# When the carried row is taken, and for how many chunks an x row is gathered ahead

## The chip, the core and the metric

The kernel runs on one core of one Trainium2 chip. The time is that of the whole program on the device, in microseconds. Of the kernel before there are three runs, 3502.38 to 3505.12 us, with a median of 3504.13 us.

## The reference

12,500 nodes with 256 features each, 212,500 edges sorted by destination (100,000 in both directions and one loop per node). What is computed, cut to what matters:

```
x1 = layernorm(x);  h = (x1 @ W) as 4 heads x 64;  a_src, a_dst = sums of h with two vectors, per head
alpha = leaky_relu(a_src[src] + a_dst[dst], 0.2)
alpha = exp(alpha - max over the edges of dst);  alpha /= sum over the edges of dst
out   = sum over the edges of dst of alpha * h[src]           # 12,500 x 256
x     = x + relu(layernorm(out + bias) * gamma + beta)
x     = x + mixture of experts(layernorm(x))                  # two of 8 experts for all rows, 256 -> 512 -> 256
```

## The kernel before

**First stage.** 50 pairs of blocks of 128 rows are loaded, transposed, multiplied with W and the attention columns, scaled by the row's norm and stored as a table in DRAM: 4 x (64 features and a one), a one, a_src and a_dst, 269 floats a row. While this runs, GpSimd gathers, for the first X_CHUNKS = 74 chunks, the rows of x that the last tile of the chunk needs (gather_x, L736, 128 rows of 1 KB), and SyncE stores them, three chunks at a time, in the DRAM tensor x_src (store_x, L534). pair_ahead(c) says which pair's transposes (tick T* of TensorE) the gather of chunk c waits for: (c - 2) * 2 // 3. SyncE stores a part 5 pairs later; the parts left over are stored after the last pair.

**Second stage.** The edges lie in 119 chunks of 14 tiles of 128 edges. A step works on several chunks at once: "own" (the messages of this step's chunk), "prev" (the chunk before is closed), "ahead", "far" (later chunks are prepared) and up to five steps ahead for the x rows. Ticks in angle names: a * marks work for the chunk ahead, a ^ for the one two ahead. There are 116 full steps in a row; the loop body holds four of them. In a step:

- GpSimd (L781) gathers the table rows of the chunk ahead, one indirect DMA per tile. In the first rounds of the walk (X_ROUNDS = 17 rounds of four) it is 13 tiles (GATHERS), since the 14th tile's rows are not fetched but computed; later it is all 14. Ahead of row 0 it waits for the messages and for TensorE's expand* of three steps before, ahead of row 6 (FIRST_ROW) for TensorE's lT^ of two steps before, the transpose of the attention values of the chunk gathered last.
- The x row: SyncE loads 128 rows from x_src (xe, L573); TensorE transposes them (xT, L911) into psXT, one half in bank 5 beside the carried row, one in bank 6; ScalarE copies them (xT, L1177); in the next step TensorE multiplies with W (xrow, L901) and ScalarE writes the scaled result as the 14th tile (xrow, L1169). VectorE and ScalarE make the norm (xstat, xvar, xln, xrstd).
- ScalarE, in this order: oh_b* (one-hots, two activations, L1098), we, we_act (L1120), carry (L1125), msgs0 (8 activations, L1105), asrc^ (L1137, waits until the rows have landed), msgs (8), rexp (L1147), acc (L1151), carried (4 activations, L1155), oh* (two, L1098), xrow, xT, wself, selfm, and the small ones of two layer norms.
- VectorE: edge_v (L1437) to DMIN, LAST_*, five messages msg0 to msg4 (L1406) with r_t (L1485) ahead of msg4, then wcur^, r_sc, newseg^, r_mn, node^, r_d1, r_d, pen^ (L1504), node_v (L1508, waits for lT^), RUNMAX^, LASTMAX^, MTILE*, the one-hots ohT0^ and ohT^ (L1401) with MNODE* and AD* between, SHIFT*, merged0 to merged3 (L1553) with LO* between, den, rden, biased0 to 3 (L1573), st (L1580), mv, gam (L1588), normed, xmid (L1597).
- TensorE: nodemax* (L881), the own node's message and the last four tiles' sums (agg, L888 and L874), lT^ (L894), xrow, xT, lastT^ (L917), turned^ (14 transposes, L922), expand* (14 matmuls, L929), the sums of the first ten tiles (half, L874), router (L942), carry (L947).

The carried row: where a node's edges run over the end of a chunk, the last row of the sums (TensorE's carry, in bank 5) is taken by ScalarE (carry), rescaled with factors that VectorE makes from it (r_t, r_sc, r_mn, r_d1, r_d), of which ScalarE takes the exponential (rexp), multiplied (carried) and added to the first row of the next chunk's sums (merged0 to 3).

The order is written out by hand. Each engine counts its instructions on one semaphore (Ticks), and a wait names a tick and a step. The list of names in Ticks is the order in which an engine does them.

**Third stage.** Two experts, in 24 groups of 512 rows and one rest.

## Time and profile before

| | |
|---|---|
| median of three runs | 3504.13 us |
| the profiled execution: its own time | 3474.59 us |
| its span, first to last instruction | 3472.8 us |
| busy: TensorE, VectorE, ScalarE, GpSimd | 2494.7, 2261.4, 1741.6, 1606.7 us |
| mean granted clock of TensorE | 0.855 |
| table gathers of GpSimd | 1594, 958 ns each |

A busy time is a sum over the span. "Idle before" in a group is the time for which the engine stood still just ahead of that group's instructions, and behind the arrow stands what released most of it. "remote" means that the profile shows no releaser; "issue" that the engine waited for nothing that it shows. "L111 q" is a sequencer's count of left-out ticks. A matmul in single precision is two instructions.

### The profile page before, as it was taken

The page shows a single profiled execution, that of the slowest core. Times are in us where ns is not written, and L with a number is a line of the kernel's source. Part 1 is how long each engine was busy: PE and PEld are TensorE (multiplying, and loading weights), DVE is VectorE, ACT ScalarE, POOL GpSimd, SP SyncE. Part 2 cuts the span into 40 slices and gives each one's busy share as a digit, 9 for nine tenths or more (in the row PEclk, how much of TensorE's full clock was granted, in tenths as well). Part 3 has the DMA queues.
Part 4 walks back from the last instruction along what each step waited for, and adds up shares of the span by engine and source line. Part 5 has one row for each costly group of instructions (what it writes and reads, how often), then busy time and mean ns, then how long its engine had stood idle before and what let it go on. Part 6 is the DMA issues. An engine that isn't in the chain of part 4 may idle for free. (4 is left out here: it accounts for less than half of the span.)

```text
span 3472.8 us, 66576 instructions
## 1 busy us (share of the span) xinstructions
PE 2494.7 (72%) x13162; PEld 1809.5 (52%) x13162; DVE 2261.4 (65%) x9525; ACT 1741.6 (50%) x5715; POOL 1606.7 (46%) x1689
## 2 busy tenths in 40 slices
PE   7746666766666766666666666666666699999998
PEld 6534445555554555454444444444444466666666
DVE  5446676766766667676666666666666655655555
ACT  4436666666665666665655555555555422222221
POOL 5465555655655656555666666666666000000000
PEclk9858888887778888888888888888888799999999
DMA  8944444444444444444444444444445201111110
GB/s 282 325 130 129 130 136 133 134 134 131 133 131 129 135 135 134 131 133 131 133 130 130 132 131 131 132 133 133 132 130 128 68 31 37 39 39 38 37 36 33
DMA packets 238971, 415.86 MB, mean 120 GB/s; under 512 B 67998, under 2 KB 153502, under 8 KB 238878
## 3 DMA queue, kind: packets, MB, share of 16 engines
q0 software_dynamic: 80064, 229.34, 24.9%
q1 hardware_dynamic: 157462, 184.01, 16.3%
q10 hardware_dynamic: 1351, 1.62, 0.2%
q14 instruction: 79, 0.64, 0.1%
q8 instruction: 15, 0.25, 0.0%
HBM read 361.68 MB, written 53.13 MB: 119 GB/s over the span
## 5 line engine op out<-in xcount | busy, mean ns | idle before, releaser
L781 POOL DMA_INDIRECT rows<-table,idx x1594 | 1526.3, 958 | 1008.6 <-issue 404.0
L874 PE MATMUL bank<-msg,oh 128*128 128x260 f32 x3332 | 984.7, 451 | 115.4 <-issue 99.4
L874 PEld LDWEIGHTS bank<-msg,oh 128*128 128x128 f32 x3332 | 750.5, 230 | 287.8 <-issue 134.1
L1105 ACT ACTIVATE msg<-rows,we 128x65 f32<-128x65 f32 x1904 | 478.6, 333 | 0.4
L1406 DVE TENSOR_TENSOR msg<-rows,bank 128x520 f32<-128x520 f32 x595 | 382.3, 677 | 0.6 <-DVEq L111 0.3
L992 PE MATMUL bank<-rows,msg 128*128 128x256 f32 x1536 | 340.6, 378 | 0.0
L979 PE MATMUL bank<-rows 128*128 128x512 f32 x768 | 335.8, 595 | 2.6 <-DMA rows<-in_L_ffn_W 2.6
L1098 ACT ACTIVATE oh_b<-bank 128x896 bf16<-128x896 bf16 x238 | 205.3, 914 | 244.3 <-remote 226.4
L922 PE MATMUL bank<-ident_b,ohT 128*128 128x128 bf16 x1666 | 178.8, 289 | 199.0 <-DVE acc L1553 52.0
L1241 ACT ACTIVATE msg<-bank,b_sb 128x512 f32<-128x512 f32 (+1 forms) x200 | 134.4, 679 | 364.4 <-PE bank L979 346.7
L992 PEld LDWEIGHTS bank<-rows,msg 128*128 128x128 f32 x1536 | 288.4, 189 | 51.4 <-issue 10.3
L922 PEld LDWEIGHTS bank<-ident_b,ohT 128*128 128x128 bf16 x1666 | 149.7, 133 | 219.8 <-issue 124.2
L979 PEld LDWEIGHTS bank<-rows 128*128 128x128 f32 x768 | 146.0, 190 | 178.1 <-issue 174.0
L1125 ACT ACTIVATE carry<-bank 1x265 f32<-1x265 f32 x119 | 45.5, 382 | 375.9 <-remote 131.9
L894 PE MATMUL bank<-ident,asrc 128*70 128x128 f32 x238 | 60.1, 340 | 220.1 <-ACT asrc L1137 133.1
L1098 ACT ACTIVATE oh<-bank 128x896 f32<-128x896 bf16 x238 | 200.9, 891 | 0.9 <-PE bank L881 0.8
L917 PE MATMUL bank<-ident,lastmax 70*128 70x70 f32 x238 | 65.4, 370 | 182.8 <-DVE lastmax L1517 180.6
L881 PE MATMUL bank<-last_p,oh_b 128*128 128x15 bf16 x1666 | 61.1, 171 | 175.3 <-DVE last_p L1472 59.5
L1202 ACT ACTIVATE ln<-mv,eps 128x1 f32<-128x1 f32 x119 | 35.1, 295 | 280.6 <-DVE mv L1584 155.6
L881 PEld LDWEIGHTS bank<-last_p,oh_b 128*128 128x128 bf16 x1666 | 50.2, 97 | 238.2 <-ACT bank L1119 114.0
L1508 DVE TENSOR_REDUCE node_v<-bank 128x70 f32<-128x210 f32 x119 | 44.7, 376 | 197.4 <-remote 91.1
L1437 DVE TENSOR_REDUCE edge_v<-bank 128x112 f32<-128x336 f32 x119 | 60.0, 504 | 171.2 <-remote 164.0
(223 smaller groups left out, 4108.8 us busy)
## 6 DMA issues: line engine op xcount, KB each, us to landing
dst_b<-dst SPq DMA_DIRECT2D x121, 448.0 KB
rows<-table,idx POOLq DMA_INDIRECT x1594
tab_w<-table SPq DMA_DIRECT2D x120, 134.5 KB
x_w<-in_x_rows SPq DMA_DIRECT2D x120, 128.0 KB
x_mid<-x_o SPq DMA_DIRECT2D x119, 128.0 KB
table<-msg SPq DMA_DIRECT2D x50, 269.0 KB
rows<-x_mid SPq DMA_DIRECT2D x26, 512.0 KB, 3.9
msg<-in_x_rows SPq DMA_DIRECT2D x51, 256.0 KB
```

Of the source, the lines that this page charges most:

```text
L781: pool.indirect_dma_start(rows[:, slot, t, :], None, table, bass.IndirectOffsetOnAxis(ap=idx[slot][:, t:t + 1], axis=0), bounds_check=None ...
L874: mm = pe.matmul(psA, oh[:, of, t, :], msg[:, of, t, :], start=(t == 0), stop=(t == TILES - 1))
L881: mm = pe.matmul(psM[:, t * 3 * R5:(t + 1) * 3 * R5], oh_b[:, t, :], last_p[:, t, :, :].rearrange("p a r -> p (a r)"), start=True, stop=True)
L894: pe2.mark("lT^", pe.matmul(psT, asrc[:, :], ident[:, :], start=True, stop=True))
L917: pe2.mark("lastT^", pe.matmul(psR, lastmax[:, :], ident[0:SR, 0:SR], start=True, stop=True))
L922: mm = pe.transpose(ps[:, c:c + P], ohT[:, s, t, 0:P], ident_b[:, :])
L979: mm = pe.matmul(u, w1_sb[:, e, k, fk * P:(fk + 1) * P], fxT[:, at.slot(), k, :], start=(k == 0), stop=(k == KD - 1))
L992: mm = pe.matmul(psY[q // 2][:, q % 2, :], hT[:, f, q * P:(q + 1) * P], w2_sb[:, e, fk, :], start=(f == 0), stop=(f == 2 * KF - 1))
L1098: ins = act.activation(to[:, i * half:(i + 1) * half, :], psO[i].rearrange("p (t n) -> p t n", n=P), ACT.Copy)
L1105: ins = act.activation(head_cols(msg[:, s, t, :])[:, h, :], head_cols(rows[:, at.slot(), t, 0:HC1])[:, h, :], ACT.Copy, scale=we[:, t, h:h ...
L1241: act3.mark(HID[f], act.activation(hT[:, f, 0:n], psU[f % len(psU)][:, 0:n], ACT.Gelu, bias=b1_sb[:, e, fk:fk + 1]))
L1406: mark(own, name, lambda: dve.tensor_tensor(msg[:, s, t:t + 2, :].rearrange("p t (h c) -> p t h c", h=H), rows[:, s4, t:t + 2, 0:HC1].rear ...
```

## The change

Three things are done.

1. All 119 chunks have an x row: X_ROUNDS and X_CHUNKS go; GpSimd gathers 119 x tiles in the first stage, paced by pair_ahead(c) = (c - 2) * PAIRS // chunks; x_src has 119 chunks; every step gathers 13 tiles and makes its 14th. The loop over the steps becomes one where there were two.
2. On ScalarE, carry moves from ahead of msgs0 to behind oh*, and rexp and carried behind it; acc and oh* keep their places behind msgs. On VectorE, r_t moves from ahead of msg4 to behind MTILE*, r_sc behind ohT0^, r_mn behind MNODE*, r_d1 and r_d behind AD*.
3. psXT's first half moves from bank 5 (where psC is) to bank 3 (where psE is). TensorE's transposes xT wait no longer for ScalarE's carry, expand* waits for ScalarE's xT of the same step, and TensorE's carry waits no longer for it.

```diff
-    X_ROUNDS = (3 * PAIRS // 2 - 5) // RING
-    X_CHUNKS = X_ROUNDS * RING + 6
-        x_src = nc.dram_tensor("x_src", [X_CHUNKS * P, D], F32, kind="Internal").ap()
+        x_src = nc.dram_tensor("x_src", [chunks * P, D], F32, kind="Internal").ap()
...
-            ... st_m msg0 mv_m msg1 msg2 msg3 r_t msg4
-            wcur^ r_sc newseg^ r_mn node^ r_d1 r_d pen^ NODE_V* RUNMAX^ NOHAS* LASTMAX^ MTILE* ohT0^ MNODE* AD* MAXSELF* ohT^ ZN*
+            ... st_m msg0 mv_m msg1 msg2 msg3 msg4
+            wcur^ newseg^ node^ pen^ NODE_V* RUNMAX^ NOHAS* LASTMAX^ MTILE* r_t ohT0^ r_sc MNODE* r_mn AD* r_d1 r_d MAXSELF* ohT^ ZN*
...
-        psXT = [bank[5][:, 320:320 + P], bank[6][:, 328:328 + P]]
+        psXT = [bank[3][:, 352:352 + P], bank[6][:, 328:328 + P]]
...
-            with nc.Fori(0, X_ROUNDS, engines=[eng.engine], hint_back_edge=long) as k:
-                four(k, step, 5)
-            hold(eng, s_nested)
-            with nc.Fori(X_ROUNDS, SURE, engines=[eng.engine], hint_back_edge=long) as k:
-                four(k, step, 2)
+            with nc.Fori(0, SURE, engines=[eng.engine], hint_back_edge=long) as k:
+                four(k, step)
...
-            return (c - 2) * 2 // 3
+            return (c - 2) * PAIRS // chunks
...
-                n_tiles = GATHERS if hi > 2 else TILES
-                for t in range(n_tiles):
+                for t in range(GATHERS):
...
                     dve2.wait(pe, MSGS[-1], at)
-                    act2.wait(pe, "carry", at)
                     act2.wait(pe, "xT", at, -1)
                     for k in range(KD):
                         mm = pe.transpose(psXT[k], xe[:, at.slot(4, 2), k * P:(k + 1) * P], ident[:, :])
...
                 if ahead:
+                    if to_turn:
+                        act2.wait(pe, "xT", at)
                     dve2.wait(pe, "LO*", at)
...
                     act2.wait(pe, "carry", at)
-                    act2.wait(pe, "xT", at)
                     pe2.mark("carry", pe.matmul(psC, ...))
...
-                if before:
-                    pe2.wait(act, "carry", at, -1)
-                    act2.mark("carry", act.activation(carry[:, :], psC, ACT.Copy))
                 (msgs0, asrc^, msgs as before)
                 if prev:
-                    dve2.wait(act, "r_d", at)
-                    act2.mark("rexp", act.activation(r_f[:, :], r_d[:, :], ACT.Exp))
                     pe2.wait(act, "agg", at)
                     dve2.wait(act, "biased3", at, -1)
                     pe2.wait(act, "carry", at, -1)
                     act2.mark("acc", act.activation(acc[:, 0:HC1], psA, ACT.Copy))
+                if ahead:
+                    pe2.wait(act, "agg", at)
+                    act2.mark("oh*", copy_one_hots(oh[:, q, :, :]))
+                if before:
+                    pe2.wait(act, "carry", at, -1)
+                    act2.mark("carry", act.activation(carry[:, :], psC, ACT.Copy))
+                if prev:
+                    dve2.wait(act, "r_d", at)
+                    act2.mark("rexp", act.activation(r_f[:, :], r_d[:, :], ACT.Exp))
                     (carried as before)
-                if ahead:
-                    pe2.wait(act, "agg", at)
-                    act2.mark("oh*", copy_one_hots(oh[:, q, :, :]))
```

## Rows read from the trace of the kernel before

**Rows 1.** The page's 40 slices: busy tenths of TensorE and of the DMA engines.
```profile
PE   7746666766666766666666666666666699999998
DMA  8944444444444444444444444444445201111110
```

**Rows 2.** Stretches of the first stage: busy by engine, clock, DMA share.
```profile
20.00:150.00 130.00, 114.39 (x571) 91.64 (x570) 79.50 (x266) 74.98 (x277) 69.85 (x70) 0.96 0.96 332
150.00:222.00 72.00, 18.20 (x108) 12.78 (x107) 12.99 (x49) 13.30 (x44) 37.04 (x39) 0.58 0.57 176
```

**Rows 3.** Groups, the x gathers: count | busy us, mean ns | idle before.
```profile
L736 POOL DMA_INDIRECT rows<-in_x_rows,oh x74 | 70.3, 950 | 67.9 <-PE bank L807 47.1 <-issue 13.7 <-DMA oh<-in_src_tiles 4.5
```

**Rows 4.** Line of edge_v: ns, first and last start; early, late steps.
```profile
L1437 DVE TENSOR_REDUCE edge_v<-bank x73: 497/500/508, 222.4 to 1749.1; 128x112 f32<-128x336 f32 x73
L1437 DVE TENSOR_REDUCE edge_v<-bank x45: 506/508/508, 1749.1 to 2689.6; 128x112 f32<-128x336 f32 x45
```

**Rows 5.** Groups, GpSimd's gathers: early steps, one more releaser, late steps.
```profile
L781 POOL DMA_INDIRECT rows<-table,idx x833 | 799.8, 960 | 559.6 <-issue 205.1 <-PE bank L894 172.3 <-remote 134.6
  PE bank L911: 33.6, 19
L781 POOL DMA_INDIRECT rows<-table,idx x588 | 561.2, 954 | 336.5 <-issue 153.6 <-remote 97.2 <-PEq L111 85.7
```

**Rows 6.** Timeline, step at 1006 us: start, duration, instructions [idle before].
```profile
1006.20 0.51 DVE L1437 TENSOR_REDUCE edge_v<-bank 128x112 f32<-128x336 f32 x1
1007.61 0.61 PE L947 MATMUL bank<-acc,sel 128*1 128x265 f32 x2
1009.83 1.92 PE L874 MATMUL bank<-msg,oh 128*128 128x260 f32 x8
1011.35 0.95 POOL L781 DMA_INDIRECT rows<-table,idx  x1 [0.30 <-issue]
1012.95 0.38 ACT L1125 ACTIVATE carry<-bank 1x265 f32<-1x265 f32 x1 [4.71 <-PE bank L874]
1015.15 0.25 ACT L1137 ACTIVATE asrc<-rows 128x70 f32<-128x70 f32 x1
1016.19 0.38 DVE L1508 TENSOR_REDUCE node_v<-bank 128x70 f32<-128x210 f32 x1 [1.21 <-PE bank L894]
1016.43 0.94 POOL L781 DMA_INDIRECT rows<-table,idx  x1 [4.13 <-PE bank L894]
1018.56 1.69 ACT L1098 ACTIVATE oh<-bank 128x896 f32<-128x896 bf16 x2
1019.56 0.47 DVE L1553 SCALAR_TENSOR_TENSOR acc<-acc,r_f,r_c 1x65 f32<-1x65 f32 x2
1021.09 0.50 PE L929 MATMUL bank<-adsh_p,ohT 128*128 128x24 bf16 x14
```

**Rows 7.** Timeline of a late step, TensorE's lT^ and GpSimd's row 6.
```profile
2225.90 0.44 PE L894 MATMUL bank<-ident,asrc 128*70 128x128 f32 x2 [1.49 <-issue]
2228.34 0.94 POOL L781 DMA_INDIRECT rows<-table,idx  x1 [2.02 <-PEq L111]
```

**Rows 8.** Groups, ScalarE's carry, 64 early and 42 late steps.
```profile
L1125 ACT ACTIVATE carry<-bank 1x265 f32<-1x265 f32 x64 | 24.5, 382 | 254.0 <-remote 114.3 <-PE bank L874 90.0 <-PE bank L881 38.9
L1125 ACT ACTIVATE carry<-bank 1x265 f32<-1x265 f32 x42 | 16.1, 383 | 90.9 <-PE bank L881 70.3 <-PE bank L874 7.9 <-PE bank L947 7.7
```

**Rows 9.** Groups, VectorE's waits: four of early steps, one of late.
```profile
L1485 DVE TENSOR_SCALAR r_t<-carry 1x1 f32<-1x1 f32 x64 | 8.9, 139 | 80.5 <-ACT carry L1125 66.5 <-issue 14.0
L1508 DVE TENSOR_REDUCE node_v<-bank 128x70 f32<-128x210 f32 x64 | 24.1, 376 | 80.2 <-PE bank L894 44.9 <-PE bank L911 31.3 <-PE bank L901 3.4
L1580 DVE BATCH_NORM_STATS2 st<-o 128x6 f32<-128x256 f32 x64 | 27.4, 427 | 104.2 <-remote 82.6 <-DVE o L1573 18.3 <-issue 3.2
L1588 DVE SCALAR_TENSOR_TENSOR o<-o,mv,g_aff 128x256 f32<-128x256 f32 x64 | 31.0, 484 | 89.2 <-remote 55.2 <-DVE mv L1584 21.6 <-issue 8.0
L1437 DVE TENSOR_REDUCE edge_v<-bank 128x112 f32<-128x336 f32 x42 | 21.3, 508 | 128.6 <-remote 128.6
```

More of the change, by code:

```diff
@@ L303, in build @@
         wide = flat_rows[:, 0:EP].bitcast(I32)
[L304 removed]
+        x_idx = flat_oh[:, 0:chunks * TILES].bitcast(I32)
         assert 2 * EP <= GATHERS * TW
[L306 removed]
+        x_parts = [slice(i, min(i + X_BATCH, chunks)) for i in range(0, chunks, X_BATCH)]
         x_ring = X_SLOT * (RING - 1) // X_BATCH
@@ L367, in build @@
         FIRST_ROW = 6
-        act2 = Ticks(sem("act2"), """oh_b* we we_act carry msgs0 asrc^ msgs rexp acc carried oh* xrow xT wself selfm ln2 y2 lhs ln1 y1 xln xrstd""", 6)
+        act2 = Ticks(sem("act2"), """oh_b* we we_act msgs0 asrc^ msgs acc oh* carry rexp carried xrow xT wself selfm ln2 y2 lhs ln1 y1 xln xrstd""", 6)
         pe2 = Ticks(sem("pe2"), "nodemax* agg lT^ xrow xT lastT^ turned^ expand* half router carry", 6)
@@ L478, in x_rows_out @@
         def x_rows_out(part):
-            return (x_src.rearrange("(q i) d -> q (i d)", i=X_CHUNKS)[:, part.start * D:part.stop * D],
+            return (x_src.rearrange("(q i) d -> q (i d)", i=chunks)[:, part.start * D:part.stop * D],
                     flat_rows[:, bass.ds(stage(part.start), (part.stop - part.start) * D)])
@@ L740, in _ @@
             pool.wait_ge(s_xidx, 16)
-            for c in range(X_CHUNKS // 3):
+            for c in range(chunks // 3):
                 gather_x(c)
@@ L744, in _ @@
             pool.tensor_scalar(narrow, wide, float(TOP16), None, ALU.min).then_inc(s_narrow, 1)
-            for c in range(X_CHUNKS // 3, X_CHUNKS):
+            for c in range(chunks // 3, chunks):
                 gather_x(c)
@@ L1158, in step @@
                 else:
-                    act2.skip(act, ["rexp", "acc", "carried"], at)
-                if ahead:
-                    pe2.wait(act, "agg", at)
-                    act2.mark("oh*", copy_one_hots(oh[:, q, :, :]))
-                else:
-                    act2.skip(act, ["oh*"], at)
+                    act2.skip(act, ["rexp", "carried"], at)
                 if to_row:
@@ L1520, in step @@
                     mtile[:, :, :], node_v[:, :, 1:R5], over(nohas[:, :], H), ALU.add))
+                if prev:
+                    act2.wait(dve, "carry", at)
+                mark(prev, "r_t", lambda: dve.tensor_scalar(r_t[:, :], carry[:, HAS:HAS + 1], BIG, -BIG, ALU.mult, ALU.add))
                 if far:
@@ L1525, in step @@
                 mark(far, "ohT0^", lambda: one_hots(0))
+                done("r_t")
+                mark(prev, "r_sc", lambda: dve.tensor_scalar(r_sc, carry[:, SHIFT:HAS], r_t[:, 0:1], None, ALU.add))
                 done("MTILE*")
```

58 lines of the change are left out of this document (25 added, 33 removed).

## The prediction

> **What bounds the kernel now.** I read the slices of the page first. The time falls into three stages: about 2 slices with the DMA engines nearly full, some 29 slices at half a DMA load with TensorE at six to seven tenths, and 8 slices of dense layers in which TensorE is full [rows 1]. The change touches the first stage (x rows gathered ahead) and the second (116 steps); the third keeps its code, so it costs and gives nothing.
>
> First stage. From 20 to 150 us the DMA share is 0.96 at 332 GB/s, while TensorE has 114 of 130 us busy and GpSimd 70 [rows 2]. The bytes are the bound. The 74 x gathers are in there [rows 3].
>
> Second stage. A step is the distance between two edge_v: (1749.1 - 222.4) / 72 = 21.20 us where GpSimd gathers 13 tiles and the x row is made on TensorE, (2689.6 - 1749.1) / 44 = 21.38 us where it gathers 14 [rows 4]. The mean of the 116 is 21.27. What a step is made of is read best from GpSimd, which issues all its gathers in one queue and stops twice a step: ahead of row 0 (it waits for expand*) and ahead of row 6 (for lT^). Over the 64 early steps its busy time is 799.8 / 64 = 12.50, "issue" 205.1 / 64 = 3.20, the stop at row 0 ("remote") 134.6 / 64 = 2.10, the stop at row 6 (172.3 + 33.6) / 64 = 3.22; sum 21.0. Late: 561.2 / 42 = 13.36, 153.6 / 42 = 3.66, 2.31 and 2.04; sum 21.4 [rows 5]. So GpSimd's queue with two stops is the whole step, and the late steps, all alike, are at its floor.
>
> Why it stops at all, if the tick it wants is old: a tick of TensorE reaches the others late while gathers are in flight. In the step at 1006 us the carry matmul ends at 1008.2, and ScalarE, waiting for nothing else, takes the row at 1012.95, 0.6 us after the sixth gather has been issued; in the late step row 6 starts 2.0 us after the end of lT^ (2225.90 + 0.44) [rows 6, 7]. I take it that such ticks come through when the gathers have drained, some 1.7 us after GpSimd stops. Then each stop costs about 2.0 us, and more only if lT^ itself is late.
>
> lT^ is late in the early steps because of what the change moves. ScalarE stands before carry for 254.0 / 64 = 3.97 us (late 90.9 / 42 = 2.16), and msgs0, asrc^ and so lT^ are queued behind it in order [rows 6, 8].
>
> **The change, part by part.**
>
> a) 45 more x gathers and stores. Each chunk is 128 KB gathered and 128 KB stored, 45 x 0.262 = 11.8 MB. At the 332 GB/s of this stretch: 35.5 us [rows 2]. The stores left for after the table become 4 from 2, and the index load ahead of the first gather grows with the chunks: I add 2.5 us. GpSimd is no bound while it only follows: 119 x 1.25 = 149 us of gathers against the some 180 us that the bytes then need. Taken: +38 us. Bounds: below, 20 us, if the stretch from 150 to 222 us, where the DMA share is only 0.57, takes up half; above, 84 us, if each of the 45 costs GpSimd's queue what one costs today, 70.3 / 74 + 67.9 / 74 = 1.87 us, and that queue becomes the bound [rows 3]. Nothing of it is hidden by compute, since the bytes bound the stage.
>
> The Trainium skill, page "DMA: Bandwidth & Descriptors", section "Bandwidth", lists 425 GB/s for one large transfer. By that figure the 11.8 MB would be 28 us instead of 35.5. The row, with mixed transfers of 1 to 4 KB, is nearer to this stage, so it decides.
>
> b) 44 steps lose their 14th gather. It is one issue of 0.95 + 0.30 = 1.25 us of GpSimd's queue [rows 6]: 44 x 1.25 = 55 us if GpSimd stays the bound; little (44 x (21.38 - 21.20) = 8 us) if they only become like today's early steps. Added in each is the x row: six matmuls (xrow, xT) after lT^, six activations (xrow, xT, xln, xrstd), xstat and xvar on VectorE, and one load of 128 KB on SyncE's queue, in front of load_edges, at a DMA load of four to five tenths [rows 1]. Today's early steps hold all of it, and all of it lies beside GpSimd's queue there; if that cover goes, VectorE's loop below is the price.
>
> c) ScalarE no longer stands before carry: msgs0 follows we_act at once. asrc^ then comes at edge_v + 4.1 instead of + 9.0 in the step at 1006 us (1015.15 - 1006.20), and lT^ is held by TensorE's own agg sums, which end at 1011.75, edge_v + 5.6 [rows 6]. GpSimd reaches row 6 at edge_v + 6.1 and the drain ends at about + 7.8. So lT^ is there in time, and the stop falls from 3.22 to the floor of 2.0: -1.2 us in an early step, 0 in a late one, whose stop is at its floor already.
>
> The floor of all 116 new steps is then 12.50 + 3.20 + 2.10 + 2.04 = 19.85 us.
>
> d) The carried row in the second half. On ScalarE acc, oh* (1.69), carry (0.38) now go in this order, and acc waits for the tick of agg, which comes with that of lT^. From this point X (node_v starts there too): acc to X + 0.4, oh* to + 2.1, carry to + 2.5. VectorE does NODE_V to MTILE by + 1.1 and stands before r_t for 1.5 us; behind that wait are queued ohT0^, MNODE*, ohT^, and on these TensorE's turned^, SyncE's load_dst. r_t to r_d with one one-hot half between them, 1.5 us: + 4.1. ScalarE: rexp 0.2 and carried 1.05: + 5.5. merged0 starts at + 5.6, where the step at 1006 us has it at 1019.56 - 1016.19 = + 3.4 [rows 6, 8]. So VectorE's second half starts 2.2 us later after X; X itself is 1.2 (early) earlier or more. VectorE stands today 1.26 us at r_t, 1.25 at node_v, 1.63 at st and 1.39 at gam in an early step [rows 9], and in a late one 3.06 at edge_v. The first two go; the last two are waits in the drain before row 0, so lateness of 2 us partly falls into them. VectorE's own loop: 21.2 - 1.26 - 1.25 + 1.5 = 20.2 us.
>
> e) expand* now also waits for ScalarE's xT, since psXT[0] lies in bank 3. xrow and xT on ScalarE follow carried: 0.6 + 0.4, to X + 6.6; expand* at X + 6.8 against + 4.9 today (1021.09). GpSimd's drain before row 0 ends at X + 10.5, so row 0 doesn't see it. But half starts 2 us later: 20 matmuls of 0.24 us, as agg's 8 in 1.92 [rows 6], are 4.8 us, and up to twice that while the granted clock is at its lower level; then router, carry, nodemax*, agg, lT^, about 5 us in all, from router to the end of agg in the step at 1006 (1006.9 to 1011.75). So X + 16.6 to X + 21.4 to the next lT^, with 18.7 in the middle, under 19.85 by 1.2 us. This slack is thin.
>
> Sum of a step: floor 19.85, VectorE's loop 20.2, TensorE's 18.7; three near loops joined by late ticks don't run at the longest one's length in each step. I take 20.5 us, between 20.2 and today's worse steps. 72 x (21.20 - 20.5) = -50; 44 x (21.38 - 20.5) = -39; first stage +38: -51 us. Both ends: 19.85 gives 116 x 1.42 = -165 + 38 = -127; 21.6 (nothing absorbed of d) gives +38 + 38 = +76.
>
> The profiled execution took 3474.6 us (span 3472.8), 29.5 below the median of the runs, 3504.1. The sum on it gives 3423.6; I carry the difference over to the median: **3453 us**.
>
> **The rivals.**
>
> R1, slower: the carried row becomes the end of the step. Place: carry, r_t, r_d, rexp, carried, xT, expand* in a chain of three hand-overs behind X, with nothing to absorb them. For it: the handovers are in the stretch in which gathers are in flight, and st and gam show VectorE's ticks are slow there too [rows 9]. Against: 3 us of standing at edge_v in late steps. Price: a step of 21.4: 116 x 0.13 + 38 = +53, 3557 us. It decides from a step of 21.27 - 38 / 116 = 20.94 us on.
>
> R2, the reorder is worth nothing: the wait of carry turns into one as long at r_t, steps stay at 21.20. Then only b's 8 us stand against 38: +30, 3534 us. For it: the waits named add up to a step whose parts all end at ticks of the same drain. Against: the late steps at their floor, which show that an early lT^ does cut the stop.
>
> R3, lT^ comes before GpSimd reaches row 6 and its tick gets through, so one stop goes wholly: 19.85 - 2.04 = 17.8, held up by VectorE's 20.2 less its drain waits, about 19.3. 116 x 1.97 = -228 + 38 = -190: 3314 us. Against: no tick of TensorE is taken at row 6 in under 1.7 us in these rows.
>
> R4, GpSimd's queue bounds the first stage (its upper end) with the forecast's steps: 3453 + 84 - 38 = 3499 us.
>
> **How the numbers follow.** Forecast 0.47 (own range 3405 to 3490, steps 20.1 to 20.8); R1 0.22; R2 0.13; R3 0.08; R4 0.10. A measurement of this kernel can tell 0.2%, 7 us, from no change. Forecast and R3 are faster but for an edge, R4 just beyond the bound for most of its spread or on it; together 0.62. The same: 0.05. Slower: R1 and most of R2, 0.33. The range 3390 to 3555 leaves out R3 and half of R1's upper part.
>
> **What would show it.** First edge_v at about 260 instead of 222.4. The idle of ScalarE before msgs none, before acc up to 3 us. GpSimd's stop at row 6 at 2.0 us in nearly all steps (right for c); one over 3 us, with lT^ behind agg and half: TensorE's loop binds. The stop at row 0 over 2.3, or VectorE not standing at st and gam and yet a step over 21: R1. r_t's wait near 1.5 us: d. Wrong would be a first stage under 20 or over 84 us longer, or steps outside 19.85 to 21.6.

## The result, and where the time went

The changed kernel takes 3551.48 us (median of four, 3536.66 to 3563.05) against 3503.87: 1.0133 of before, 95% interval 1.0102 to 1.0164. Slower by 1.3%, where 3453 was forecast. Times compared in this document are of runs in one and the same state of speed; a slower one showed only once (3592.90 us, one of the four runs of e7_old_row8), and the ratio of that run is without it. The profiled execution has a span of 3534.8 us, 62.0 more than before, and a mean granted clock of 0.823 (before 0.855).

The page's slices of the changed kernel:

```profile
PE   7736766667676766667777667676776699999998
PEclk9867877877777778877777777778777799999999
DMA  8964444444444444444444444444444211111110
```

They have the shape of [rows 1]; the stretch of half a DMA load is longer. Split by edge_v over the whole run, before and changed (the group's line, as in [rows 4]), and by stretch, as in [rows 2]; the first of the stretches is of the kernel before:

```profile
L1437 DVE TENSOR_REDUCE edge_v<-bank x119: 497/507/508, 222.4 to 2722.7; 128x112 f32<-128x336 f32 x119
L1430 DVE TENSOR_REDUCE edge_v<-bank x119: 494/501/509, 268.3 to 2783.7; 128x112 f32<-128x336 f32 x119
```

```profile
222.00:980.00 758.00, 515.53 (x3060) 387.71 (x3061) 524.90 (x2345) 466.30 (x1640) 447.31 (x467) 0.81 0.47 131
20.00:150.00 130.00, 94.44 (x430) 74.11 (x429) 61.79 (x205) 55.87 (x210) 82.44 (x85) 0.89 0.90 309
150.00:265.00 115.00, 48.66 (x251) 36.99 (x249) 32.18 (x111) 31.53 (x110) 65.84 (x70) 0.70 0.72 235
1000.00:1750.00 750.00, 520.17 (x3036) 389.30 (x3035) 529.94 (x2313) 468.14 (x1618) 435.68 (x456) 0.79 0.47 132
```

The first edge_v comes at 268.3 instead of 222.4: +45.9. A step is (2783.7 - 268.3) / 118 = 21.32 us, before it was (2722.7 - 222.4) / 118 = 21.19 over the same 118: +15. So of the 62 us between the two profiled executions three quarters are the first stage, and the steps, from which 89 us were to come, took 15 more. The two executions don't lie alike among their runs: the one before is 29.3 us under its median (3503.87 - 3474.59), the changed one 14.8 under (3551.48 - 3536.66). Between the medians the loss is 47.6 us, and the first stage's 45.9 are nearly all of it. That the steps didn't give their 89 us is certain; whether they took 15 is not.

What a step is made of now. GpSimd's gathers, and VectorE's groups that answer to [rows 9] (the last line is den in the kernel before):

```profile
L772 POOL DMA_INDIRECT rows<-table,idx x852 | 814.0, 955 | 587.6 <-issue 210.6 <-PE bank L884 166.6 <-remote 85.8
```

```profile
L1580 DVE SCALAR_TENSOR_TENSOR o<-o,mv,g_aff 128x256 f32<-128x256 f32 x119 | 58.2, 489 | 4.4
L1572 DVE BATCH_NORM_STATS2 st<-o 128x6 f32<-128x256 f32 x119 | 50.9, 428 | 55.9 <-remote 35.5 <-DVE o L1565 17.5
L1490 DVE TENSOR_REDUCE node_v<-bank 128x70 f32<-128x210 f32 x119 | 43.9, 369 | 39.5 <-PE bank L884 33.1 <-PE bank L900 2.4 <-PE bank L891 2.2
L1558 DVE TENSOR_SCALAR rden<-acc 128x4 f32<-128x4 f32 x119 | 21.2, 178 | 226.2 <-remote 193.5 <-DVE acc L1545 20.8 <-issue 10.4
L1505 DVE TENSOR_SCALAR r_t<-carry 1x1 f32<-1x1 f32 x119 | 16.6, 139 | 58.0 <-ACT carry L1144 41.6 <-issue 6.9 <-ACT oh L1088 6.1
L1566 DVE TENSOR_SCALAR rden<-acc 128x4 f32<-128x4 f32 x119 | 20.3, 170 | 4.1
```

GpSimd's line is of 300 to 1700 us, 852 / 13 = 65.5 steps: 12.4 us busy, 3.2 "issue", and (587.6 - 210.6) / 65.5 = 5.8 for all the rest, nearly all of it the two stops, where the forecast had 4.1 and [rows 5] give, counted alike, (559.6 - 205.1) / 64 = 5.5. Taken gather by gather from the timeline of 400 to 1600 us, the stop ahead of row 6 is 3.40 us (3.25 before) and the one ahead of row 0 is 2.26 (2.12 before). VectorE's standing at r_t, node_v, st and gam fell from 5.5 us a step (the early steps of [rows 9]) to (58.0 + 39.5 + 55.9 + 4.4) / 119 = 1.3 us. But in front of den (the first line whose output is rden, L1558) it now stands 226.2 / 119 = 1.9 us, where before it stood 4.1 us in the whole run. The rest is in small waits. In all VectorE stands as long as before: its busy share in the stretch from 1000 to 1750 is 529.94 / 750, so it stands 0.293 x 21.32 = 6.3 us a step (before, from 222 to 980 us, it was busy 524.9 of 758 us: 6.5).

One step of the changed kernel, timeline (start, duration, instructions, idle before), and TensorE's work up to the next lT^:

```profile
996.38 0.50 DVE L1430 TENSOR_REDUCE edge_v<-bank 128x112 f32<-128x336 f32 x1
1000.67 0.25 ACT L1122 ACTIVATE asrc<-rows 128x70 f32<-128x70 f32 x1
1002.04 1.92 PE L864 MATMUL bank<-msg,oh 128*128 128x260 f32 x8
1003.80 0.38 PE L884 MATMUL bank<-ident,asrc 128*70 128x128 f32 x2
1004.45 0.95 POOL L772 DMA_INDIRECT rows<-table,idx  x1 [3.74 <-PE bank L884]
1005.14 0.37 DVE L1490 TENSOR_REDUCE node_v<-bank 128x70 f32<-128x210 f32 x1
1006.03 0.37 ACT L1144 ACTIVATE carry<-bank 1x265 f32<-1x265 f32 x1
1006.42 0.14 DVE L1505 TENSOR_SCALAR r_t<-carry 1x1 f32<-1x1 f32 x1
1009.39 0.53 DVE L1545 SCALAR_TENSOR_TENSOR acc<-acc,r_f,r_c 1x65 f32<-1x65 f32 x2
1010.28 0.47 DVE L1545 SCALAR_TENSOR_TENSOR acc<-acc,r_f,r_c 1x65 f32<-1x65 f32 x2
1011.97 0.95 POOL L772 DMA_INDIRECT rows<-table,idx  x1 [0.30 <-issue]
1013.10 0.55 PE L920 MATMUL bank<-adsh_p,ohT 128*128 128x24 bf16 x14 [2.72 <-remote]
1013.49 7.22 PE L864 MATMUL bank<-msg,oh 128*128 128x260 f32 x20
1014.51 0.17 DVE L1558 TENSOR_SCALAR rden<-acc 128x4 f32<-128x4 f32 x1 [3.77 <-remote]
1015.12 0.95 POOL L772 DMA_INDIRECT rows<-table,idx  x1 [2.21 <-PE bank L920]
1018.21 0.50 DVE L1430 TENSOR_REDUCE edge_v<-bank 128x112 f32<-128x336 f32 x1
1022.51 1.92 PE L864 MATMUL bank<-msg,oh 128*128 128x260 f32 x8
1024.26 0.38 PE L884 MATMUL bank<-ident,asrc 128*70 128x128 f32 x2
```

Look at the two L1545 and at L1558. den waits for nothing but VectorE's own tick of merged3, which ended at 1010.75; it starts at 1014.51, 1.6 us after GpSimd has issued its seventh gather (1011.97 + 0.95). expand* starts at 1013.10, 0.2 us after that gather, though what it waits for (LO* and ScalarE's xT) ended by 1010.4. In the semaphore events of this stretch VectorE's counter goes up at 1010.17, 1011.61, 1013.05, 1013.78 and 1014.49, 0.7 or 1.4 us apart; in the first two gathers behind row 6 it still went up within 0.1 us of an instruction's end (node_v ends at 1005.51, the counter goes up at 1005.52). That is the prediction's late tick, met here by TensorE and by VectorE with itself.

Look at TensorE too. From expand* at 1013.10 it works without a gap: half to 1020.71, then router, carry, nodemax*, the own message, agg from 1022.51, and lT^ to 1024.64, for which GpSimd stands. So in this step the late expand* makes the next lT^ late. Over the 55 steps of the timeline from 400 to 1600 us it is 13.4 us from expand* to the end of lT^, of which TensorE stands 1.7 (before: 15.6 and 4.4); the stop ahead of row 6 is over 3 us in 24 of 55. The prediction had named that as the sign of TensorE's loop.

### The profile page after: what moved, and what is told of

Read it like the earlier page. It is cut to its first block and busy times, and to the rows that moved or that the text cites. A ratio compares the mean times of both kernels' runs of the same rounds, so it can differ in the third digit from the quotient of the medians.

```text
span 3534.8 us, 67560 instructions
## 1 busy us (share of the span) xinstructions
PE 2622.9 (74%) x13450; PEld 1910.6 (54%) x13450; DVE 2320.3 (66%) x9621; ACT 1824.7 (52%) x6003; POOL 1600.2 (45%) x1687
## 5 line engine op out<-in xcount | busy, mean ns | idle before, releaser
L772 POOL DMA_INDIRECT rows<-table,idx x1547 | 1477.0, 955 | 1064.7 <-issue 384.8
L864 PE MATMUL bank<-msg,oh 128*128 128x260 f32 x3332 | 1085.8, 494 | 2.7 <-DVEq L111 1.4
L864 PEld LDWEIGHTS bank<-msg,oh 128*128 128x128 f32 x3332 | 834.5, 255 | 183.7 <-issue 2.1
L911 PE MATMUL bank<-ident_b,ohT 128*128 128x128 bf16 x1666 | 163.2, 273 | 274.7 <-DVE zn L1528 72.3
L911 PEld LDWEIGHTS bank<-ident_b,ohT 128*128 128x128 bf16 x1666 | 136.4, 125 | 292.0 <-issue 243.3
L1088 ACT ACTIVATE oh_b<-bank 128x896 bf16<-128x896 bf16 x238 | 205.3, 914 | 32.0 <-remote 20.5
L920 PE MATMUL bank<-adsh_p,ohT 128*128 128x24 bf16 x1666 | 64.9, 182 | 202.3 <-remote 84.2
L891 PE MATMUL bank<-wx,xeT 128*128 128x260 f32 x480 | 143.9, 425 | 80.9 <-DVE msg L1399 64.5
L920 PEld LDWEIGHTS bank<-adsh_p,ohT 128*128 128x128 bf16 x1666 | 53.4, 104 | 227.6 <-remote 106.7
L1558 DVE TENSOR_SCALAR rden<-acc 128x4 f32<-128x4 f32 x119 | 21.2, 178 | 226.2 <-remote 193.5
L1394 DVE TENSOR_SCALAR ohT<-dst_b,node 128x896 bf16<-128x896 int16 x238 | 159.9, 672 | 5.7 <-DVEq L111 0.5
```

The costliest lines, as they stand in the source:

```text
L772: pool.indirect_dma_start(rows[:, slot, t, :], None, table, bass.IndirectOffsetOnAxis(ap=idx[slot][:, t:t + 1], axis=0), bounds_check=None ...
L864: mm = pe.matmul(psA, oh[:, of, t, :], msg[:, of, t, :], start=(t == 0), stop=(t == TILES - 1))
L891: mm = pe.matmul(psXR, xeT[:, k, :], wx[:, k, 0:D + H], start=(k == 0), stop=(k == KD - 1))
L911: mm = pe.transpose(ps[:, c:c + P], ohT[:, s, t, 0:P], ident_b[:, :])
L920: mm = pe.matmul(psE[:, t * 6 * H:(t + 1) * 6 * H], ohT[:, q, t, 0:P], adsh_p[:, :, :].rearrange("p a r -> p (a r)"), start=True, stop=True)
L1088: ins = act.activation(to[:, i * half:(i + 1) * half, :], psO[i].rearrange("p (t n) -> p t n", n=P), ACT.Copy)
```

## The experiments

Eighteen runs. In the first eight the kernel before took 3494 to 3501 us beside them, as in the result: machine A. In the last ten it took 2962 to 2965 beside them, and the waits "remote" of 2 us are not in those traces: machine B. The names stand for two groups of chips: the record numbers the chips 6 (e1 to e4) and 13 (e5 to e8) in A, 3 (e9 to e12), 15 (r1 to r4) and 4 (r5, r6) in B. What differs between the groups is not shown. Ratios are to the kernel before on the same chip.

| run | change | machine | us | ratio, interval | step, us |
|---|---|---|---|---|---|
| e1_x119 | 119 x rows, old order | A | 3524.61 | 1.0088 (1.0067 to 1.0108) | 21.23 |
| e2_order | new order, 74 x rows | A | 3548.14 | 1.0154 (1.0130 to 1.0177) | 21.72 |
| e3_bank5 | changed, psXT in bank 5 | A | 3545.26 | 1.0144 (1.0120 to 1.0167) | 21.34 |
| e4_x119_asrc | e1, carry behind asrc^ | A | 3532.41 | 1.0104 (1.0082 to 1.0127) | 21.31 |
| e5_row8 | changed, stop at row 8 | A | 3508.68 | 1.0024 (1.0006 to 1.0042) | 21.07 |
| e6_row4 | changed, stop at row 4 | A | 3720.48 | 1.0633 (1.0610 to 1.0657) | 22.81 |
| e7_old_row8 | e1, stop at row 8 | A | 3565.27 | 1.0128 (1.0075 to 1.0181) | 21.62 |
| e8_warm | changed, idle matmuls | A | 3636.28 | 1.0386 (1.0362 to 1.0410) | 22.17 |
| r1_after | the changed kernel | B | 3004.44 | 1.0143 (1.0126 to 1.0160) | 17.29 |
| r2_x119 | as e1 | B | 2941.31 | 0.9924 (0.9908 to 0.9941) | 16.69 |
| e9_x18, r3_x18 | before, 18 x rows | B | 3010.35, 3010.78 | 1.0166, 1.0157 | 17.49, 17.52 |
| e11_norow6, r4_norow6 | changed, no stop at lT^ | B | 2999.11, 2998.93 | 1.0127, 1.0121 | 17.12, 17.14 |
| e10_stop10 | changed, a third stop | B | 3319.71 | 1.1206 (1.1187 to 1.1225) | 19.84 |
| e12_thin | changed, half the rows of 7 gathers | B | 2996.74 | 1.0118 (1.0101 to 1.0135) | 17.12 |
| r5_carry_asrc | as e4 | B | 2925.23 | 0.9872 (0.9855 to 0.9888) | 16.53 |
| r6_carry_oh | changed, carry ahead of oh* | B | 2924.86 | 0.9877 (0.9860 to 0.9893) | 16.48 |

A step is the distance from first to last edge_v over 118, in the one profiled execution. That execution can lie up to 15 us off the median (e2 13.9 under it, r1_after 15.5 over), which is 0.13 us a step, so differences of steps under 0.2 us are not to be trusted without the medians.

### The parts of the change: e1, e2

```diff
# e1: the whole diff, but the order of ScalarE and VectorE, and psXT, as before
# e2: before, with the changed order, psXT in bank 3 and its waits
-  we_act carry msgs0 asrc^ msgs rexp acc carried oh* xrow
+  we_act msgs0 asrc^ msgs acc oh* carry rexp carried xrow
```

> Only the x rows of all 119 chunks; the carried row is taken as in the kernel before (ahead of the messages, psXT in bank 5). Theory A (the loss of the changed kernel is its longer first stage, +46 us at the first edge_v, and the reorder gives and takes nothing): first edge_v at 266 to 270, steps 21.2 in the whole run, 3504 + 46 - 8 = 3542. Theory B (the reorder itself makes steps longer, the x rows cost only the first stage): the same 3542 or below, and the changed kernel is slower than this one by 10 us or more. Theory C (what was forecast: today's early steps are held by the carry ahead of asrc^): steps of 21.2, 3542, and the reorder ought to have been 70 us better than this.

> Only the reorder and psXT in bank 3; 74 chunks have an x row. Theory A: 3504, within 0.2 %. Theory B (the carried row's chain, taken late, ends in the stretch with gathers in flight, so merged0 to den and expand* come late and GpSimd's stop at row 6 is held by TensorE): steps 21.35 to 21.5 among the first 72, 3515 to 3530; its stop at row 6 near 3.3 us as in the changed kernel. If late steps without x row (no xT in front of expand*) are below 21.0 here, the x row's copies ahead of expand* are the cause, not the carried row.

edge_v and VectorE's st of e1; then edge_v of e2, whole and in its late steps:

```profile
L1427 DVE TENSOR_REDUCE edge_v<-bank x119: 495/500/509, 265.6 to 2770.4; 128x112 f32<-128x336 f32 x119
L1570 DVE BATCH_NORM_STATS2 st<-o 128x6 f32<-128x256 f32 x119 | 50.9, 428 | 267.8 <-remote 259.2 <-DVE o L1563 5.6 <-issue 2.5
```

```profile
L1440 DVE TENSOR_REDUCE edge_v<-bank x119: 494/500/509, 217.6 to 2780.7; 128x112 f32<-128x336 f32 x119
L1440 DVE TENSOR_REDUCE edge_v<-bank x44: 494/500/509, 1777.2 to 2742.9; 128x112 f32<-128x336 f32 x44
```

The x rows alone cost 31 us between the medians of one chip (3524.61 - 3493.79), of which the first stage is 43. By the profiled executions nothing comes back in the steps (21.23 against 21.19), by the medians some 12 us, although 44 of them have a gather less. In e1 VectorE stands 267.8 / 119 = 2.3 us ahead of st, again for its own tick: the same wait as den's, at another place of its chain. The order alone costs 54 us, most of it in late steps: (2742.9 - 1777.2) / 43 = 22.46 us against 21.38 [rows 4]. Its steps with x rows take 21.34 (217.6 to 1754.4 over 72), as theory B had them. Theory A (only the first stage) falls with e2, and theory B's 3515 to 3530 is missed by the late steps, in which VectorE stands 117.5 / 40 = 2.9 us at st. The sum 31 + 54 is not the change's 48: an x row step takes 21.2 to 21.3 in either order, a 14-gather step takes the new order badly. Theory C, the forecast's, falls too: the reorder on top of e1 made the kernel 16 (by the ratios) to 27 us (by the medians) slower, which is theory B's "10 us or more", and not 70 faster.

### Where the carried row and psXT stand: e3, e4

```diff
# e3
-        psXT = [bank[3][:, 352:352 + P], ...
+        psXT = [bank[5][:, 320:320 + P], ...      # xT waits for carry, expand* no longer for xT
# e4: e1, and on ScalarE
-  we_act carry msgs0 asrc^ msgs
+  we_act msgs0 asrc^ carry msgs
```

> The changed kernel with psXT's first half back in bank 5 and the waits that go with it (xT waits for ScalarE's carry, expand* for nothing of ScalarE's xT). Theory W (the new wait of expand* on ScalarE's xT is what lengthens TensorE's loop): expand* 1.5 to 3 us earlier after node_v, steps 20.6, 3551 - 80 = 3470. Theory B (late chain; LO* and the ticks of VectorE are as late as xT): within 0.3 % of 3551.

> All 119 chunks have an x row, the order of the kernel before but for one thing: ScalarE takes the carried row behind asrc^ instead of ahead of msgs0; VectorE's r_ chain stands where it stood before, psXT in bank 5. If what gains is that ScalarE no longer stands in front of asrc^ (the forecast's step c) and what loses is the late chain: lT^ as early as in the changed kernel, merged0 as early as before, stop at row 6 of 2.0, steps 20.3 to 20.8, 3440 to 3500 with the first stage's 46. If the stop at row 6 is no matter of the carried row at all (theory A): 3542.

VectorE's den and TensorE's expand* of e3, then VectorE's den of e4:

```profile
L1558 DVE TENSOR_SCALAR rden<-acc 128x4 f32<-128x4 f32 x119 | 20.5, 172 | 244.1 <-remote 196.1 <-issue 24.5 <-DVE acc L1545 22.9
L919 PE MATMUL bank<-adsh_p,ohT 128*128 128x24 bf16 x1666 | 65.8, 182 | 194.4 <-remote 104.3 <-DVE acc L1545 65.5 <-DVE adsh_p L1554 18.6
```

```profile
L1556 DVE TENSOR_SCALAR rden<-acc 128x4 f32<-128x4 f32 x119 | 20.3, 171 | 174.9 <-remote 165.8 <-DVE acc L1543 4.1 <-issue 3.1
```

Without its wait for xT, expand* stands 194.4 / 119 = 1.6 us ahead of it (1.7 in the changed kernel): theory W falls, and theory B's "within 0.3% of 3551" holds: bank 3 costs nothing. e4 has the r_ chain where it was and ScalarE's asrc^ ahead of carry, misses its 3440 to 3500 as the forecast missed, and stands 1.5 us at den. With 13 gathers and the stop at row 6, the step on machine A (21.23 to 21.34) doesn't care for the place of the carried row.

### The loop through GpSimd's bursts: e5, e6, e7

FIRST_ROW is the row ahead of which GpSimd waits for lT^; it sets the pace of the gathers and nothing else.

```diff
-        FIRST_ROW = 6
+        FIRST_ROW = 8          # e5, e7 (on e1); 4 in e6
```

> The changed kernel with FIRST_ROW = 8: GpSimd waits for lT^ ahead of row 8 instead of row 6, so 5 gathers instead of 7 lie between lT^ and the end of the queue. Theory L (the step is a loop: lT^, seven gathers of 1.25 us, then VectorE's own tick comes through at den, 4.8 us of VectorE to the next edge_v, 6.9 us to the next lT^): two gathers less in the loop, it becomes 18.9, and GpSimd's own 16.3 + 2.2 + 2.0 = 20.5 takes over; steps 20.3 to 20.8, 3551 - 100 = 3450. Theory G (GpSimd's queue with its two stops is the step, as forecast): nothing changes but where the stop is, 3551 within 0.3 %. Theory P (TensorE's low clock holds lT^): the same, 3551.

> The changed kernel with FIRST_ROW = 4: nine gathers behind lT^. Theory L: the loop grows by two gathers, 2.5 us a step: 23.5 to 23.9, 3551 + 116 x 2.4 = 3830. Theories G and P: 3551 within 0.5 %.

> The run with the old order and 119 x rows (3525), with FIRST_ROW = 8. Theory L: its loop is lT^, seven gathers, VectorE's tick at st, 3.5 us to edge_v, 9.3 to row 6; with five gathers it is 18.8, so GpSimd's 20.5 takes over here too: 3430 to 3450, and the orders are equal within 10 us. If the lateness of lT^ (8.6 after edge_v, behind the carried row) costs by itself, the old order stays 40 us or more behind the new one.

VectorE in e5, in e6, and ScalarE's carry and TensorE's lT^ in e7:

```profile
L1558 DVE TENSOR_SCALAR rden<-acc 128x4 f32<-128x4 f32 x119 | 21.0, 176 | 78.9 <-DVE acc L1545 73.0 <-remote 3.2 <-issue 1.5
```

```profile
L1572 DVE BATCH_NORM_STATS2 st<-o 128x6 f32<-128x256 f32 x119 | 50.9, 428 | 388.0 <-remote 280.1 <-issue 107.7
```

```profile
L1115 ACT ACTIVATE carry<-bank 1x265 f32<-1x265 f32 x119 | 45.5, 382 | 622.6 <-remote 449.4 <-PE bank L864 95.7 <-PE bank L871 42.9
L884 PE MATMUL bank<-ident,asrc 128*70 128x128 f32 x238 | 70.2, 390 | 398.4 <-ACT asrc L1127 336.6 <-issue 37.1 <-ACT msg L1095 18.1
```

Theories G and P, by which nothing changes, fall: five gathers behind lT^ instead of seven give 0.25 us a step (0.36 by the medians), nine cost 1.49. The sign is theory L's, the sizes are some third and six tenths of its 0.9 and 2.4, so a loop "lT^, burst, late tick, lT^" is part of the step and not all of it. Whether it closes through VectorE's tail, as theory L has it, or through TensorE's expand*, half and agg, these runs don't tell apart: both wait for the burst. With five, the wait at den is down to 0.7 us, and with nine VectorE stands 3.3 us at st. e7 misses theory L's 3430 to 3450 and meets its other case, the old order 40 us or more behind the new one. ScalarE stands 622.6 / 119 = 5.2 us ahead of the old carry (436.5 / 119 = 3.7 in e1), and lT^ comes behind; that the longer burst ahead of row 8 makes this tick later is argued, not shown. There, and only there on machine A, the new order is the better one (1.0024 against 1.0128), though e7's runs spread from 3531 to 3593 us.

### The clock: e8

```diff
+                    for i in range(8):       # ahead of nodemax*
+                        pe.matmul(bank[5][:, 320:320 + P], ident_b[:, :], ident_b[:, :], ...)
...
+                    act2.wait(pe, "carry", at)
+                    for i in range(24):      # ahead of expand*
+                        pe.matmul(bank[5][:, 320:320 + P], ident_b[:, :], ident_b[:, :], ...)
```

> The changed kernel with useless bf16 matmuls on TensorE where it stands: 8 ahead of nodemax* and 24 ahead of the wait for expand*. Theory P (TensorE stands 2 to 4 us ahead of expand* and nodemax*, its granted clock falls, half takes 7.2 us and agg 3.7 instead of 4.8 and 1.9, and this holds lT^ and so the stop at row 6): mean granted clock back to 0.85 or more, lT^ at edge_v + 5.9 in most steps instead of 6.9, steps shorter by 0.5 to 1 us, 3440 to 3500. Theory L with lT^ at its median: at most 1 us of lT^ is to be won, and only in the steps in which agg is slow. If the clock rises and the time stays, the clock was not on the path.

```profile
L864 PE MATMUL bank<-msg,oh 128*128 128x260 f32 x3332 | 1031.8, 475 | 13.8 <-ACT msg L1102 9.1 <-issue 2.9 <-DVEq L111 1.4
L921 PE MATMUL bank<-ident_b 128*128 128x128 bf16 x2808 | 257.4, 271 | 2.5 <-ACT carry L1151 2.5
L1497 DVE TENSOR_REDUCE node_v<-bank 128x70 f32<-128x210 f32 x119 | 44.8, 377 | 253.3 <-PE bank L887 251.7 <-DVEq L111 1.5
```

The forecast of 3440 to 3500 is missed. The clock went from 0.823 to 0.848 and a sums matmul from 494 ns to 475, but the idle matmuls stand in TensorE's order, 257.4 / 119 = 2.2 us a step, and VectorE stood 2.1 us for lT^ (0.3 in the changed kernel). The wait for ScalarE's carry that came with them cost 2.5 us in the whole run. TensorE's slack is as thin as the forecast had it; that the clock itself costs nothing is not shown, since this run could not pay for it.

### Machine B: e9 to e12, r1 to r4

```diff
# e9, r3: before, X_ROUNDS = 3
# e11, r4: changed, FIRST_ROW = 13 (never)
# e10: changed, and ahead of row 10
+                        pool.wait_ge(s_rows[slot], ...)     # the ten gathers before have landed
# e12: changed, rows 6 to 12 over 64 partitions; half of their table rows are left out
```

> The kernel before with X_ROUNDS = 3: x rows for 18 chunks only, 56 fewer, the old order. Price of an x row in the first stage: from the 45 more of the run with 119 (first edge_v 265.6 against 222.4) 0.96 us each; if that holds downwards too, first edge_v at 170 to 175. Theory N (an x row gains nothing in the steps: 13 gathers and the x row's work take as long as 14 gathers, 21.2 to 21.4): 104 steps of 21.38, 3501 - 50 + 8 = 3459. If the x rows did gain the 14th gather's 1.25 us in a step: 3501 - 50 + 70 = 3521. If the first stage is bound by something else below 74 x rows (TensorE is busy 114 of 130 us there): first edge_v at 200 or later, 3490 or more.

> The changed kernel with a third stop of GpSimd: ahead of row 10 it waits until its ten gathers before have landed. Theory G (GpSimd's queue with its stops is the step): one stop of 2.0 to 2.3 us more, steps 23.4, 3551 + 235 = 3785. Theory T (the step is VectorE's chain, whose own ticks come through slowly from some 4 us of gathers in a row on, 0.7 us apart, and GpSimd has slack that it spends at row 6): with bursts of 6, 4 and 3 gathers VectorE stands less than 0.7 us ahead of den instead of 2.0, GpSimd's stop at row 6 shrinks, and the time is 3551 within 2 %.

> The changed kernel without the stop for lT^ (FIRST_ROW = 13, which never comes): 13 gathers in one burst. Theory G: the queue becomes 16.3 + 2.2 = 18.5 and VectorE's loop of about 20 takes over, 3400. Theory T: a burst of 16 us, in which VectorE's 15.1 us of work and its own ticks run slowly; standing moves from den to other places, and steps stay at 21 or above, 3530 or more.

> The changed kernel with seven of the 13 gathers (rows 6 to 12 of a step) over 64 partitions instead of 128, so that half of their rows keep what an earlier step left: part of the computation is left out. It asks whether the number of rows on their way slows the ticks. Theory T by traffic: half the packets behind row 6, VectorE's wait ahead of den falls from 2.0 to under 1 us, and steps to 20.5 or below whatever the issue costs. If an issue still costs 0.95 + 0.30 and the wait ahead of den stays, it is the issuing that slows the ticks, not the rows. If an issue gets shorter, GpSimd's queue falls too, and by theory G steps fall by seven times what an issue loses.

> The changed kernel itself once more, to set beside the last four runs, on whose chip the kernel before took 2962 us and not 3504. If the chip is the slower one: 1.013 of before, as in the result. If it is the faster one, two theories. Theory T (what costs is that ticks come through slowly in a burst of gathers; the faster chip does not have that, GpSimd does not stand at row 6 there, and 13 gathers follow each other): steps are GpSimd's queue or VectorE's work, 17.1 to 17.5; with the first stage at 224 it is 0.99 to 1.013 of before. Theory G (fourteenth gather and early lT^ are worth what was forecast where nothing else slows): 0.96 to 0.98 of before.

> The old order with x rows for all 119 chunks. On the slower chip 1.009 of before, as measured. On the faster one: if the reorder is what lengthens or shortens steps, this differs from the changed kernel by more than 10 us; if not, the two are within 10 us.

> The kernel before with x rows for 18 chunks. On the faster chip it was 1.0166 of before, so there an x row gains in a step more than it costs in the first stage. On the slower chip, theory N (13 gathers and an x row take as long as 14 gathers): first edge_v at 170 to 185, steps 21.3 to 21.4, 3455 to 3470, 0.985 to 0.992 of before. If an x row gains there too: 1.00 or more.

> The changed kernel without GpSimd's stop for lT^. On the faster chip 1.0127 of before. On the slower one, theory G: the queue is 16.3 + 2.2 = 18.5 and VectorE's loop of about 20 takes over, 3400, 0.97 of before. Theory T: one burst of 13 gathers, in which VectorE's own ticks are slow from its fourth microsecond on; steps of 21 or more, 3530 or more, 1.008 or more.

The numbers of microseconds in these texts are for machine A; only the ratios of the last four were for either. Of these, r1's 1.0143 stands just above theory T's 0.99 to 1.013 and far from theory G (0.96 to 0.98), and r2 lies 63 us under r1 where 10 was the mark: the reorder itself costs here. The changed kernel on machine B: edge_v, a stretch, VectorE's waits, and a step's timeline around den:

```profile
L1430 DVE TENSOR_REDUCE edge_v<-bank x119: 497/500/508, 226.2 to 2266.1; 128x112 f32<-128x336 f32 x119
1000.00:1750.00 750.00, 595.94 (x3723) 453.91 (x3720) 648.91 (x2861) 577.84 (x1994) 536.19 (x564) 0.84 0.59 163
L1558 DVE TENSOR_SCALAR rden<-acc 128x4 f32<-128x4 f32 x119 | 20.3, 170 | 4.1
L1505 DVE TENSOR_SCALAR r_t<-carry 1x1 f32<-1x1 f32 x119 | 16.9, 142 | 116.5 <-ACT carry L1144 113.8 <-DVEq L111 2.7
```

```profile
1013.95 0.14 DVE L1505 TENSOR_SCALAR r_t<-carry 1x1 f32<-1x1 f32 x1 [0.75 <-ACT carry L1144]
1017.35 0.47 DVE L1545 SCALAR_TENSOR_TENSOR acc<-acc,r_f,r_c 1x65 f32<-1x65 f32 x2
1017.85 0.17 DVE L1558 TENSOR_SCALAR rden<-acc 128x4 f32<-128x4 f32 x1
```

The same program, the same burst of gathers: den starts at 1017.85, 0.03 us after merged3. VectorE stands (1 - 648.91 / 750) x 17.29 = 2.3 us a step, 4.0 less than on machine A, and the step is 4.0 us shorter (21.32 - 17.29). Its work being the same, the second follows from the first; what tells more is where it stands less. From 300 to 1700 us its waits ahead of REST*, LO*, den, rden, biased0 to 3 and st, nearly all for its own ticks or "remote", are (15.2 + 14.3 + 130.8 + 24.0 + 20.9 + 31.7) / 65.5 = 3.6 us a step on machine A and 14.9 / 81 = 0.2 on machine B. So waits of the kind of the late tick are most of the 4 us: that is the strongest reading here. It stays a comparison of chips and not of one thing changed. Other things differ with it: half takes 7.2 us in the step shown on A and 6.0 us in the one on B, and the stretch from 20 to 150 us moves 309 GB/s and 375.

On machine B the queue of GpSimd is near the step: 14 gathers x 1.25 = 17.5, and e9 and r3, whose steps nearly all have 14, measure 17.49 and 17.52; there an x row is worth having (r2's steps are 16.69). At the third stop of e10 GpSimd stands 427.8 / 119 = 3.6 us, its other stops shrink by 0.9, and the step grows by 19.84 - 17.29 = 2.55 us, near the 2.0 to 2.3 that theory G has and far from theory T; on machine A it was not run. Taking the stop at lT^ away (e11, r4) gives next to nothing: 5 us between the medians of r1 and r4, and their intervals overlap; the 0.15 us between the steps is mostly r1's long profiled execution. Half the rows in seven gathers (e12, 934 ns an issue instead of 952) gives as little, so on machine B the bytes of the gathers aren't the bound. Whether row count or issuing slows the ticks on machine A isn't told, since e12 did not run there.

### The changed order mended: r5, r6

```diff
# r6: changed, on ScalarE
-  acc oh* carry rexp carried
+  acc carry oh* rexp carried
```

> All 119 chunks with an x row and the carried row taken directly behind asrc^, VectorE's r_ chain where it was. On the slower chip it was 1.010 of before. On the faster one, theory V (there a step is VectorE's 14.9 us of work and its waits, of which the old order has 0.7 at node_v behind a late lT^ and the changed one 1.0 at r_t): both waits are gone here, steps fall from 16.67 to GpSimd's 13 x 1.25 = 16.3, 2941 - 43 = 2898, 0.978 of before. If lT^ is not what VectorE waits for: 0.992, like the old order.

> The changed kernel with ScalarE's carry ahead of oh* instead of behind it; all else as in the changed kernel. On the faster chip, theory V: VectorE's wait ahead of r_t, 0.96 us a step, goes (carry is there 1.7 us earlier), oh* comes 0.4 us later; steps 17.26 become 16.4 to 16.8, 0.98 to 0.995 of before. If the wait is not the price of the reorder: 1.014. On the slower chip, theory T: the wait of 0.46 ahead of r_t goes and comes back ahead of den; 1.013 within 0.3 %.

VectorE's r_t in r2 (old order), r5 and r6, and node_v in the first two:

```profile
L1475 DVE TENSOR_SCALAR r_t<-carry 1x1 f32<-1x1 f32 x119 | 16.6, 140 | 32.4 <-ACT carry L1115 28.9 <-issue 2.1
L1498 DVE TENSOR_REDUCE node_v<-bank 128x70 f32<-128x210 f32 x119 | 44.5, 374 | 98.3 <-PE bank L884 97.9 <-DVEq L111 0.4
```

```profile
L1475 DVE TENSOR_SCALAR r_t<-carry 1x1 f32<-1x1 f32 x119 | 16.8, 141 | 159.6 <-ACT carry L1128 157.3 <-ACT asrc L1122 2.1
L1498 DVE TENSOR_REDUCE node_v<-bank 128x70 f32<-128x210 f32 x119 | 42.5, 357 | 11.1 <-PE bank L884 10.7 <-PEq L111 0.3
```

```profile
L1505 DVE TENSOR_SCALAR r_t<-carry 1x1 f32<-1x1 f32 x119 | 16.5, 139 | 36.0 <-ACT carry L1139 33.3 <-DVEq L111 2.5
```

One activation moved ahead of two: the wait ahead of r_t falls from 116.5 to 36.0 us in the run, the step from 17.29 to 16.48 and the time from 3004 to 2925 us, 1.2% under the kernel before (2964.54 on that chip). Theory V said 0.98 to 0.995 for r6, and 0.9877 was measured. So on machine B the loss of the change is this one place, oh* (1.7 us) ahead of carry. r5 ends within 1 us of it; both are near 13 x 1.25 = 16.3 us of GpSimd. r5 still stands 1.3 us at r_t, so theory V's "both waits are gone" is wrong for it, and its 0.978 is missed; that GpSimd's queue hides this wait is argued from the nearness of 16.53 to 16.3. On machine A, r5's kernel is e4, 1.0104, and r6 was not run.

## Why the prediction was wrong

The step that failed is c): that with carry out of its way lT^ is there when GpSimd reaches row 6, so that the stop falls from 3.22 to 2.0 us. It is 3.40. With it failed the term "VectorE's loop: 20.2", which takes 2.5 us of waits out of VectorE's step and puts 1.5 back; VectorE's standing stayed at 6.3 us.

- **What bounds the kernel** [rows 5 to 7]: that GpSimd's queue with two stops is the step, and that ticks come late while gathers are in flight. The second is right and was priced at GpSimd's stops alone. VectorE's waits at st and gam, 1.63 and 1.39 [rows 9], were in the rows, most of them "remote"; I read them as slack that lateness may fall into. They are the same delay, met wherever the chain is when the burst is on.
- **a)** +38 forecast, +45.9 measured, inside its bounds. The stretches that take the bytes run at 309 and 235 GB/s, not at 332. On machine B the price is less: from r3 to r2 223.4 - 192.9 = 30.5 us for 101 chunks. The figure of the Trainium skill, page "DMA: Bandwidth & Descriptors", section "Bandwidth", 425 GB/s, was farther off still.
- **b)** The 14th gather was to give 44 steps room to fall from 21.38 to 20.5, 39 us. e1's steps are 21.23 with 13 gathers in all of them, which is 44 x 0.15 = 7 us, the 8 us of the case in which they only become like the early ones. On machine B it is worth 17.5 - 16.7 = 0.8 us a step.
- **c)** asrc^ comes at edge_v + 4.3, as forecast, and ScalarE stands 4.1 us in the whole run before its messages. But lT^ ends at edge_v + 7.6 in the mean (9.1 before), where agg's end at + 5.6 was taken: in the step shown TensorE is at half, router and carry until + 4.8, and nodemax* and agg follow. And GpSimd reaches row 6 at edge_v + 4.5 (6.6 before), where + 6.1 was taken, since edge_v, at the end of a tail that starts with the late den, comes later in GpSimd's round. In the step shown lT^ ends at 1004.18 and GpSimd had stood since 1000.71. So lT^ came 1.5 us earlier after edge_v and GpSimd 2.1 us earlier.
- **d)** The chain X, r_t, merged0 was forecast at + 5.6 and is + 4.3 in the step shown (1009.39 - 1005.14), r_t waits 0.49 us and not 1.5. All of that is better than forecast and worth nothing, because den then waits 1.9 us. The waits at r_t and node_v fell to 0.49 and 0.33 us, near what was said; the time came back at den and behind it. On machine B, where den doesn't wait, r_t's wait is 1.0 us and is the price of the change there.
- **e)** In the step shown expand* is at X + 8.0 (forecast 6.8), half takes 7.2 us (4.8, up to twice that), and the next lT^ ends at X + 19.5, where 18.7 was forecast as the middle of 16.6 and 21.4 (that middle is 19.0) against a floor of 19.85. So TensorE's loop has no slack once its expand* is late. e3 shows that the wait for xT is not why it is late; in the step shown LO* ended at 1010.36, 2.7 us ahead of it.
- **The rivals.** 3551 lies between R2 (3534) and R1 (3557). R1 gave a step of 21.4, and said what would show it: VectorE not standing at st and gam and yet a step over 21. That is what came (0.47 and 0.04 us, 21.32). Its place, the three hand-overs of the carried row, is wrong on machine A by e3 and e4, so its number is near by luck; it is right in kind on machine B, where r6 mends it. I gave it 0.22 since "3 us of standing at edge_v in late steps" would absorb the chain; e2's late steps, 1.1 us longer, show that they don't. R2's mechanism, the wait of carry come back at r_t, is not what happened either: the wait came back at den. R3 and R4 are out: no stop went, and the first stage stayed under its 84 us.

Open: what makes ticks slow on machine A, in a burst of gathers from the third or fourth on, and whether the number of rows or of issues matters; how much of a step there is TensorE's lower clock, which e8 could not tell; what r6 is worth there.
